# Around each unit's softplus: decay tiles two ahead, twelve scalings on VectorE, other items in those places

## The reference, cut to what matters

```
xc    = silu(conv(x @ in_proj.T) + conv_b)             # 256 channels
dt, Bm, Cm = split(xc @ x_proj.T, [64, 16, 16])
delta = softplus(dt @ dt_w.T + dt_b)
h     = h * exp(delta * A) + (delta * xc) * Bm          # for each token, 256 channels x 16 states
y     = sum over states of h * Cm, + xc * D, * silu(z), @ out_proj.T
```

## Time and profile before

| | |
|---|---|
| median of three runs | 596.76 us |
| the profiled execution | 597.98 us |
| its span, first to last instruction | 596.2 us |
| ScalarE, busy in the span | 445.2 us, 75% |
| VectorE | 466.6 us, 78% |
| TensorE | 497.6 us, 83% |
| GpSimd | 330.5 us, 55% |

### The profile page before, as it was taken

How to read it: one execution, slowest core, us unless ns; L and a number is a source line. 1 busy time by engine, 2 the same in 40 slices (tenths; PEclk the granted TensorE clock), 3 DMA queues, 4 the chain that set the end, 5 groups by cost and what they waited for, 6 DMA issues and landing times.

```text
span 596.2 us, 9244 instructions
## 1 busy us (share of the span) xinstructions
PE 497.6 (83%) x3378; PEld 409.0 (69%) x3378; DVE 466.6 (78%) x709; ACT 445.2 (75%) x847; POOL 330.5 (55%) x155
## 2 busy tenths in 40 slices
PE   3578979996899999698998896778967486999997
PEld 2245856876788678586965676678856375788696
DVE  5866887976978777699799985988999999866422
ACT  2459865999998789999975899987979761274250
POOL 3104645867966677696766777957667673200000
PEclk9888998998999999799999997979989989978999
DMA  7031120321322222123220231312272214000101
GB/s 256 0 110 37 71 71 36 101 75 38 111 85 90 74 72 71 59 87 106 73 72 35 72 107 36 111 47 95 71 212 76 86 53 142 0 1 2 35 1 36
DMA packets 17885, 43.46 MB, mean 73 GB/s; under 512 B 1328, under 2 KB 7600, under 8 KB 17584
## 3 DMA queue, kind: packets, MB, share of 16 engines
q1 hardware_dynamic: 17840, 42.87, 21.9%
HBM read 41.56 MB, written 1.31 MB: 72 GB/s over the span
## 4 chain that ended last, share of the span: by engine, by line
PE 40%; ACT 28%; DVE 23%; issue 6%; POOL 1%; DMA 1%; POOLq 0%; DVEq 0%; ACTq 0%
ACT dBuT L572 13%; PE pro L1198 11%; DVE area L984 9%; PE yT L1198 9%; PE yT L1202 8%; ACT dA L565 8%; PE dBu L1202 6%; PE dBu L1198 4%; DVE area L980 3%; PE pro L1202 2%; DVE area L772 1%; ACT pre L540 1%; ACT th L533 1%; DVE pre L954 1%; ACT area L555 1%
## 5 line engine op out<-in xcount | busy, mean ns | idle before, releaser
L481 POOL TENSOR_TENSOR hc<-area 128x1024 f32<-128x1024 f32 x127 | 303.2, 2390 | 159.6 <-DVE area L980 92.4
L572 ACT ACTIVATE dBuT<-area,bT 128x256 f32<-128x256 f32 x508 | 215.1, 498 | 13.8 <-PE dBu L1202 13.7
L1202 PE MATMUL dBu<-ident,dBuT 128*128 128x128 f32 x1024 | 147.2, 281 | 43.3 <-DVE area L984 23.5
L565 ACT ACTIVATE dA<-area,Aneg 128x1024 f32<-128x1024 f32 x128 | 146.1, 1142 | 20.3 <-DVE area L984 13.5
L1202 PEld LDWEIGHTS dBu<-ident,dBuT 128*128 128x128 f32 x1024 | 118.1, 144 | 57.3 <-issue 21.3
L1202 PE MATMUL yT<-ident,hc 128*128 128x128 f32 x1024 | 140.3, 282 | 1.7 <-POOL hc L481 1.4
L1202 PEld LDWEIGHTS yT<-ident,hc 128*128 128x128 f32 x1024 | 120.7, 145 | 20.6 <-issue 16.4
L984 DVE TENSOR_TENSOR_SCAN area<-dA,area,dBu 128x512 f32<-128x512 f32 x64 | 81.8, 1278 | 4.5
L980 DVE TENSOR_TENSOR_SCAN area<-dA,area,dBu 128x512 f32<-128x512 f32 x64 | 81.8, 1278 | 4.1
L980 DVE TENSOR_TENSOR_SCAN area<-dA,dBu 128x512 f32<-128x512 f32 x64 | 77.1, 1205 | 7.7 <-PE dBu L1202 7.0
L984 DVE TENSOR_TENSOR_SCAN area<-dA,dBu 128x512 f32<-128x512 f32 x64 | 77.1, 1205 | 6.5 <-PE dBu L1202 6.0
(11 more groups left out here) (227 smaller groups left out, 570.1 us busy)
## 6 DMA issues: line engine op xcount, KB each, us to landing
area<-c_rows SPq DMA_DIRECT2D x64, 512.0 KB, 3.7
dBuT<-w_in SPq DMA_DIRECT2D x1, 2048.0 KB, 9.2
wp<-wpack_in SPq DMA_DIRECT2D x1, 1030.0 KB, 7.5
x<-x_in SPq DMA_DIRECT2D x2, 512.0 KB, 6.5
hc<-bcast_in SPq DMA_DIRECT2D x1, 1024.0 KB, 10.5
out<-x SPq DMA_DIRECT2D x4, 256.0 KB, 2.4
hT<-w_in SPq DMA_DIRECT2D x1, 512.0 KB, 7.3
acc<-w_in SPq DMA_DIRECT2D x1, 512.0 KB, 7.5
```

Source lines behind the costliest of these rows:

```text
L481: g_.tensor_tensor(hc[:, e % 3, :], hs[:, e % 3, :], Cb[:, g % 3, :], ALU.mult).then_inc(hc_done, 1)
L565: nc.scalar.activation(dA[:, e % 3, :], delta[par][:, half, :], ACT.Exp, scale=Aneg[:, dr, half, s:s + 1]).then_inc(da_ready, 1)
L572: return nc.scalar.activation(dBuT[:, g % 2, n, :], duT[par][:, n, :], ACT.Copy, scale=bT[:, par, n, s:s + 1])
L1202: return nc.tensor.matmul(out, in_, ident[:, :] if idn is None else idn, start=start, stop=True, is_transpose=True, skip_group_check=True)
```

## The change

`schedule()` lays the items out anew and returns, for each unit, the tile of its softplus: the turn in which ScalarE handles the last DT.
- **Unit 0**: up to DT as before. Then two tiles without an item (t = 19, 20), Z at 21 to 24, DU at 25 to 28.
- **Unit 1**: O leaves t = 6 and 7 and goes to t = 19 and 20, behind DT. X1 to X3, B, BT and DT so move two tiles ahead (DT at 15 to 18). Z at 21 to 24, DU at 25 to 28.
- **Unit 2**: O stays at 6 and 7. Z0 and Z1 of unit 3 follow at 8 and 9, X1 to X3 at 10 to 15, B, B, BT at 16 to 18, DT at 19 to 22, two tiles without an item, DU at 25 to 28, Z2 and Z3 at 29 and 30.
- The softplus is at t = 19, 19 and 23 instead of 22. In its turn ScalarE makes the decays of the next **two** tiles ahead of it, and none in the turn after.
- Three chunks of four scalings in each unit pass from ScalarE to VectorE (`BY_VECTOR`, `scale_four`): VectorE does four of them behind the second scan chunk of t = SP_AT, SP_AT + 1 and SP_AT + 2. They are 12 instructions a unit, 36 in all. TensorE waits for them by a semaphore of their own, and ScalarE's counts are made without them.
- delta * xc now goes into `pre`, in place, since yg is still read by O. The norm stage at t = 30 of unit 2, which also writes there, waits for the last DU instead of the softplus.

```diff
+            turned = [(k, j, u - 1) for k, j in LAST_ITEMS[0:4]]
+            added = [(k, j, u - 1) for k, j in LAST_ITEMS[4:6]]
...
+            if u == 0:
+                items = early + [("Z", j, 0) for j in range(4)] + x + steps + [None, None] + z + turns
+            elif u + 2 < NU:
+                items = early + turned + x + steps + added + z + turns
+            else:
+                items = early + turned + added + z[0:2] + x + steps + [None, None] + turns + z[2:4]
...
+            if it[0] == "DT":
+                softplus_at[u] = at - NH * DS * u + 1
...
+BY_VECTOR = []
+for _u in range(NU - 1):
+    for _e in range(NH * DS * _u + SP_AT[_u], NH * DS * _u + SP_AT[_u] + 3):
+        BY_VECTOR.append((_e // NH + 2, 0) if _e % NH else (_e // NH + 1, 1))
...
-        du = yg
+        du = pre
...
-                if e + 1 < NT:
+                u, t = divmod(e, DS * NH)
+                ahead = u + 1 < NU and t == SP_AT[u]
+                if e + 1 < NT and not (u + 1 < NU and t == SP_AT[u] + 1):
                     exp_tile(e + 1)
+                if ahead:
+                    exp_tile(e + 2)
...
-                if e % (DS * NH) == SP_AT and g // DS + 1 < NU:
-                    softplus(g // DS + 1)
+                if ahead:
+                    softplus(u + 1)
...
+            def scale_four(g, i):
...
+                dve.wait_ge(dbu_ready, NCH * (NH * (g - 1) - 1) + freed + 1)
+                for n in range(c * BPC, (c + 1) * BPC):
+                    last = nc.vector.tensor_scalar(dBuT[:, g % 2, n, :], duT[par][:, n, :], bT[:, par, n, s:s + 1],
+                                                   None, ALU.mult)
+                last.then_inc(vector_scaled, 1)
...
                 scan_chunk(e, 1)
+                if u + 1 < NU and 0 <= e % (DS * NH) - SP_AT[u] < 3:
+                    scale_four(*BY_VECTOR[3 * u + e % (DS * NH) - SP_AT[u]])
...
-                    pe.wait_ge(dbut_ready, max(NCH * g - 1, 0) + i + 1)
+                    if (g, i) in BY_VECTOR:
+                        pe.wait_ge(vector_scaled, BY_VECTOR.index((g, i)) + 1)
+                    else:
+                        pe.wait_ge(dbut_ready, by_scalar(g, i))
```

More of the change, by code:

```diff
@@ L65, in schedule @@
 def schedule():
-    parts = [[] for _ in range(NT)]
+    parts, softplus_at = [[] for _ in range(NT)], [0] * (NU - 1)
     for u in range(NU):
@@ L70, in schedule @@
         if u + 1 < NU:
[L71 to L76, removed]
+            turned = [(k, j, u - 1) for k, j in LAST_ITEMS[0:4]]
+            added = [(k, j, u - 1) for k, j in LAST_ITEMS[4:6]]
+            early = [("X", 0, u + 1)]
+            z = [("Z", j, u + 1) for j in range(4)]
+            x = [("X", j, u + 1) for j in range(1, 4)]
+            steps = [("B", 0, u + 1), ("B", 1, u + 1), ("BT", 0, u + 1)] + [("DT", j, u + 1) for j in range(4)]
+            turns = [("DU", j, u + 1) for j in range(4)]
+            if u == 0:
[4 more added lines that the diff above has]
+                items = early + turned + added + z[0:2] + x + steps + [None, None] + turns + z[2:4]
         at = NH * DS * u
         for it in items:
+            if it is None:
+                at += 1
+                continue
+            if it[0] == "DT":
+                softplus_at[u] = at - NH * DS * u + 1
             for p in range(0, parts_of(it[0]), 2):
@@ L81, in schedule @@
                 at += 1
-        assert at <= NH * DS * (u + 1) - 2
+        assert at <= NH * DS * (u + 1) - 1
     at = NH * DS * (NU - 1)
@@ L90, in schedule @@
     ends = [[it for it, p in row if p == parts_of(it[0]) - 1] for row in parts]
-    return parts, [row[0] if row else None for row in ends]
-PARTS, ENDS = schedule()
-SP_AT = 22
+    return parts, [row[0] if row else None for row in ends], softplus_at
+PARTS, ENDS, SP_AT = schedule()
+BY_VECTOR = []
+for _u in range(NU - 1):
+    for _e in range(NH * DS * _u + SP_AT[_u], NH * DS * _u + SP_AT[_u] + 3):
+        BY_VECTOR.append((_e // NH + 2, 0) if _e % NH else (_e // NH + 1, 1))
 GATES_AT, ADD_LN_AT = 9, (11, 13)
@@ L109, in count_of, with by_scalar @@
     return sum(o[0] in kinds for o in ORDER[:NUMBER[it] + 1])
+def by_scalar(g, i):
+    return NCH * g + i + 1 - sum(c <= (g, i) for c in [(0, 1)] + BY_VECTOR)
 def product_at(e):
     u, t = divmod(e, DS * NH)
-    if u + 1 == NU or t not in (SP_AT + 1, SP_AT + 2):
+    if u + 1 == NU or t - SP_AT[u] not in (1, 2):
         return None
-    return t - SP_AT - 1
+    return t - SP_AT[u] - 1
 def build_block(nc, x_d, mod_d, wpack_d, bcast_d, dtw_d, w1_d, w2_d, crow_d, out_d):
@@ L248, in build_block @@
         dbut_ready = sem("dbut_ready")
+        vector_scaled = sem("blocks_scaled_by_vector")
         dbu_ready = sem("dbu_ready")
@@ L617, in _ @@
                 g, half = divmod(e, NH)
-                if e + 1 < NT:
+                u, t = divmod(e, DS * NH)
+                ahead = u + 1 < NU and t == SP_AT[u]
+                if e + 1 < NT and not (u + 1 < NU and t == SP_AT[u] + 1):
                     exp_tile(e + 1)
+                if ahead:
+                    exp_tile(e + 2)
                 first = g + 1 < NG and (g + 1) % DS == 0
                 if half == 0:
-                    if g + 1 < NG:
+                    if g + 1 < NG and (g + 1, 1) not in BY_VECTOR:
                         scale_blocks(g + 1, 0 if first else 1)
@@ L626, in _ @@
                         scale_blocks(g + 1, 1)
-                    if g + 2 < NG and (g + 2) % DS != 0:
+                    if g + 2 < NG and (g + 2) % DS != 0 and (g + 2, 0) not in BY_VECTOR:
                         scale_blocks(g + 2, 0)
@@ L811, in first_high_blocks @@
                 last.then_inc(high0_ready, 1)
+            def scale_four(g, i):
+                u, s = divmod(g, DS)
+                _, _, par = unit(u)
+                c = chunks(u)[i]
+                freed = list(chunks((g - 2) // DS)).index(c)
+                dve.wait_ge(dbu_ready, NCH * (NH * (g - 1) - 1) + freed + 1)
[3 more added lines that the diff above has]
+                last.then_inc(vector_scaled, 1)
             def tap_weights():
@@ L950, in norm_stage @@
                     if stage == 7 and b == 0:
-                        dve.wait_ge(delta_ready, NH * (NU - 1))
+                        wait_item(dve, "DU", 3, NU - 1)
                     dst = acc if stage == 2 else lnx
```

## The result

| | median, us | runs, us | ratio to before, with its 95% interval |
|---|---|---|---|
| before | 597.26 | 596.41 to 598.20 | |
| after | 611.97 | 606.64 to 618.45 | 1.0213 [1.0184, 1.0241] |

One of the four runs (618.45) was disturbed and is in the median but not in the ratio, and so it is with such runs in the experiments, one of 1663.76 us in the kernel with both pool_du later among them. The other three are 611.57, 612.37 and 606.64. The profiled execution is the first of them: 611.57 us, span 609.8, so 13.6 us more than the span before. By the medians the difference is 14.7 us, by the ratio 12.7. The prediction was 610.5 us, slower at 0.75, with a sum of +13.9. The kernel became slower in the way that it describes.

A forecast was written before the change was run, and what follows sets the result against it. ScalarE was taken to set the pace behind the softplus, TensorE earlier in a unit, and VectorE after the change. Units 0, 1 and 2 add 5.7 + 2.3 + 5.9 = +13.9 us, forecast 610.5 us, range 597 to 616.

The forecast's parts named there:

- A group costs 5.0, 5.2 and 3.05: Each unit's three groups of four VectorE scalings, held up by GpSimd's product and pool_du: 13.3 us a unit.
- The reading of the norm stage: Trace of eight tensor_scalar meeting a GpSimd product, first two together 2.61 us; from it a group meeting one product costs 3.05.
- The second scaling between product and pool_du: Group at SP_AT + 1: by the skill's rule its second scaling passes between both GpSimd instructions, making the group 5.03 us.
- my other figure: Group at SP_AT + 1 taken as 5.2 us, between bounds 5.03 (second scaling passes) and 5.30 (it doesn't).
- My own 4.97: First group: its fourth scaling waits for pool_du until 4.97 us after the scan's end, so the group costs 5.0.
- A Z costs 0.61: Each Z item on VectorE adds 0.69 us less 0.08 of overlap, 0.61, and an O the same.
- Early decays: Decays made two ahead let VectorE scan SP_AT + 1 and + 2 under the softplus; its waits for ScalarE go.
- TensorE's waits for VectorE's scalings: TensorE waiting for scalings moved to VectorE: no cost, since they are made two or three tiles ahead.
- The group keeps its place: Rival: a group holds GpSimd off to its end and costs 1.05 us; median 580.2 us, chance 0.12.
- only products hinder: Rival: both pool_du fall outside the groups, a unit costs 9.15 us; median 598.2 us, chance 0.12.
- one pool_du a unit: Rival: first pool_du starts after the first group's fourth scaling, that group costs 3.05 us; 604.7 us, chance 0.17.
- More than I count, by the clock: Rival: longer stalls lower TensorE's clock for the first X tiles, up to 4 us more; 614.5 us, chance 0.06.

## Why the prediction was right, step by step

- *ScalarE sets the pace before, VectorE after: shown* by the stretches above, and by the waits for tanh, 25.3 us down to 1.5.
- *A group costs 5.0, 5.2 and 3.05: measured 5.26, 5.24 and 3.14* in unit 0. The reading of the norm stage carried over to another operation and size. That the cost is the meeting with GpSimd, and not the scalings, is shown by the kernel in which GpSimd waits: the same groups cost 1.05, and it is 25 us faster. The first was 0.26 under. In unit 0 its product starts 0.28 behind the scan's end (121.02 against 120.74) where I had 0.08, so all that waits ends 0.2 later; my picture of its second scaling held up by the product was also wrong there, for it was the third. In unit 1 the product is on time (232.52), but pool_du starts at 235.02, 0.12 behind its end, and takes 2.51.
- *The second scaling between product and pool_du.* The order is the one that the Trainium skill's rule gives (SBUF — State Buffer, section Who interferes with whom): the second scaling, waiting since 128.65, ended at 131.10 although pool_du had been ready behind the product. The cost is nearer to my other figure all the same, 5.24 and not 5.03. The third scaling came just too late for the same gap and waited for the whole pool_du, and the fourth had to run after it. My own 4.97 for a group whose last scaling is stopped, with 0.26 for one more behind it, gives 5.23; my 5.03 was a slip in the sum.
- *My list of what would be seen was wrong in one line.* It had six groups with one long instruction and three with two. By my own sum the first group has two as well, and measured it is the other way about: 15 long ones, two in each of six groups and one in each of three.
- *A Z costs 0.61: measured 0.40 (2.90 - 2.50),* and an O the same (8.13 - 7.74 and 6.04 - 5.64, unit 1 against unit 0). This is the term that was mis-sized. VectorE after, one tile with a Z and one without:

```profile
142.17 1.19 DVE L1020 TENSOR_TENSOR_SCAN area<-dA,dBu 128x512 f32<-128x512 f32 x1
143.28 0.65 DVE L909 SCALAR_TENSOR_TENSOR area<-th,pro 128x512 f32<-128x512 f32 x1
143.86 1.27 DVE L1020 TENSOR_TENSOR_SCAN area<-dA,area,dBu 128x512 f32<-128x512 f32 x1
...
150.93 1.20 DVE L1020 TENSOR_TENSOR_SCAN area<-dA,dBu 128x512 f32<-128x512 f32 x1
152.23 1.28 DVE L1020 TENSOR_TENSOR_SCAN area<-dA,area,dBu 128x512 f32<-128x512 f32 x1
```

  Without a Z the second chunk (dA, area, dBu) starts 1.30 behind the first, of which it needs the last column; with one, 1.69. The scan that would follow 0.10 behind the first chunk's end (152.13, then 152.23) now starts 0.07 ahead of the end of the Z (143.93), so 0.65 of work, less 0.08 of overlap before it, adds only 0.40. In unit 0 this is 4 x 0.2 = 0.8 too much, the groups were 0.3 too little (13.64 against 13.3), and so 48.3 became 47.8. In unit 1 the same two errors (six items there) make 48.6 of 49.4, to 0.1; tiles 0 to 18 took 0.2 more than I had (63.9 against 63.7), and the sum is +1.8 instead of +2.3. In unit 2 from t = 23 I had 41.1, and it is 41.2: two errors that cancel, the groups 0.46 too little (13.76), and the two Z 0.42 too much. In the total, too, errors of both signs cancel: that it came out within 0.3 us of the span is in part luck.
- *Early decays: neither gain nor cost,* and not needed for what I credited to them. I had them as the reason why VectorE finds its decays under the softplus; without them it still finds them, for the groups keep VectorE so long that ScalarE is not late. (Where the groups are short they were not tried without.) ScalarE of the kernel with the decays one ahead, behind the softplus (a wait, but for VectorE):

```profile
121.58 2.19 ACT L589 ACTIVATE dA<-area,Aneg 128x1024 f32<-128x1024 f32 x2
...
125.26 1.15 ACT L589 ACTIVATE dA<-area,Aneg 128x1024 f32<-128x1024 f32 x1 [1.49 <-DVE area L1018]
```

- *TensorE's waits for VectorE's scalings,* put at nothing: its weight loads stood 13.1 us for them, in three places. VectorE was busy all but 1.0 us or less of each stretch, so no cost shows.
- *The rivals.* "The group keeps its place" and "only products hinder" fall with the groups' 5.26, 5.24 and 3.14; "one pool_du a unit" with the first group. "More than I count, by the clock" is not shown: the granted clock is 0.86, 0.93 and 0.81 in the three stretches (0.96, 0.91 and 0.86 before), but VectorE sets their pace, and their lengths are those of the sum without it. The clock moved single executions at other places, by 2.7 and 9.4 us.
- *What I did not see* is that the idea of the change was sound. With the layout alone the kernel is 0.7% faster than before, and with the scalings on VectorE and kept clear of GpSimd 2%. The slowdown is only the choice of the instant: layout about -3.6 us, scalings moved at 1.05 a group some -7 more (593.71 to 586.60), and the meetings with GpSimd +25.

## What to carry to other kernels

A run of short VectorE instructions that starts together with a long one of GpSimd cost here, for each GpSimd instruction that it met, what was left of it, and that was nearly all; count those in GpSimd's queue, the ones behind the first too. Price moved work with the neighbour that it will have, from a place in the trace where the two already meet, and then try the other order: a semaphore that lets the short group go first, or one instruction at a time in the gap, turned 2% slower into 2% faster here. When the kernel without the suspect part is run beside it, an edit that looks like one idea falls into parts of both signs.

## What the runs showed that I had not expected

- *One scaling passes at the end of a GpSimd instruction, a second one only by a hair.* In the second group of unit 0 the third scaling started 0.11 behind pool_du (131.02 against 130.91) and waited 2.4 us for it. In the first group of unit 1 it started 0.05 ahead (234.97 against 235.02) and took 0.34, but then the fourth waited for the same pool_du (2.44). In the first group of unit 2 it is 0.03 ahead by the records (368.62 against 368.65) and was stopped all the same, 2.52. The three groups take 5.31, 5.32 and 5.41 us: what counts is how many GpSimd instructions a group meets, and not which scaling meets them.
- *TensorE's clock differs at the same place and the same work from one profiled execution to the next:* 0.77, 0.78 and 1.00 in 80 to 95 us, 0.91 and 0.83 in the tail. To compare the whole times of one profile of each kernel would have given the early decays a cost of 3.7 us that the stretches where they act don't show.
